# A post-norm decoder layer on one core: the first sequence's feed-forward layers issued among the second sequence's attention

## The chip, the core and the metric

One core of one Trainium2 chip runs one program. The time is that of the whole program on the device, in microseconds (us). Of the kernel before, three runs are shown: 967.42, 971.66 (the median) and 973.08.

## What is computed

Two sequences of 1024 tokens with 256 features go through one decoder layer, all in float32:

```python
x = _layernorm(x + _L0_attn_ref(x, w_qkv, w_proj))            # 16 heads of 16, rope, causal
x = _layernorm(x + _L0_xattn_ref(x, ctx, ctx, mask, ...))     # 77 context positions, 16 heads
x = _layernorm(x + _L0_ffn_ref(x, ...))
# feed-forward, D_IN = 256, D_HID = 1024
h = silu(tlin(x, w1_w, w1_s)) * tlin(x, w2_w, w2_s)
h = gelu(tlin(h, h1_w, h1_s))
h = gelu(tlin(h, h2_w, h2_s))
return tlin(h, w3_w, w3_s)
```

Here tlin(x, w, s) is x @ w.T times a scale for each output, and the weights w are small whole numbers, which need few bits of the mantissa.

## The kernel before, in words

A loop of two passes (line 338) runs one sequence each; at its end stand a barrier of all engines and a clearing of the semaphores. All weights of feed-forward, 22 pieces of 4 KB a partition, lie in SBUF in `ffn_w`. One region of SBUF, the arena, is used over and over: the tiles of attention, later those of feed-forward.

A pass has four stages, and on every engine its instructions stand in one fixed order, written out by hand as numbered steps. What joins the engines is semaphores.

- **Projections.** PE makes q and k of eight token tiles (L456) and v (L463), DVE turns q and k by rope (L980 to L982), POOL adds (L1265), ACT evicts v (L849).
- **Self-attention.** Steps -20 to 57. For each pair of heads DVE and POOL split q and k in a high and a low part (L1012, L1271), PE transposes them (`turn`, L507), ACT evicts (L843). PE makes 24 blocks of scores (`max_unit`, L521) only for the maximum of each row; DVE reduces them (L1028 whole blocks, L1030 those on the diagonal). The maxima go by PE (L528), ACT and four small DMAs (L425) into extra rows of q. Then steps 0 to 47 take one block of 128 keys for four heads each: four scores (L550) into four banks, the exponential on ACT (L878), the causal cut on POOL (L1280), the values on PE (L567). The maxima of a later pair of heads are made beside the steps of an earlier one, up to step 32. From step 42 on the output projection, norm and the next queries are made tile by tile (L591, L598, L605, L615, L1085, L1099). In the first pass DVE also looks whether a weight needs more bits than a single pass of float32r holds (L1074, 22 pieces).
- **Cross-attention.** Steps -9 to 12, in the same manner with 77 keys (L638, L655, L1124, L676, L908, L1141 and L1318 for the mask, L688, L696), then the second norm, whose result DVE and ACT split into `x_hi` and `x_lo` (L894, L1147).
- **Feed-forward** (`ffn`, L715). Two chunks of 512 tokens. Each activation is split in a high part (DVE, L1164) and a low part (POOL, L1326), and every product is made with both. Groups: w1 and w2 for eight tiles of outputs (L733), h1 and h2 with sixteen matmuls a group (L749), w3 for four token tiles (L761). Silu and Gelu are ACT's (L954, L964), the gate's product DVE's (L1224). Six banks go round. The first chunk's w1 and w2 groups run beside the last four tiles of the norm of cross-attention (L737).

PE's order in one step of self-attention is this (from line 784):

```python
for j in range(4):
    if 0 <= s < LAST:
        score(s, j)
    for unit in units[j:j + 1]:
        max_unit(*unit)
    ...                       # turn, rows, y_turn
norm_products(0, s, ("yt", "proj"))
if 0 <= s - 1 < LAST:
    values(s - 1)
norm_products(0, s, ("xt", "q"))
```

Of the kernel before, what the change touches and what calls it, by code (L numbers as in the profile page):

```python
# [20 lines left out]
F32 = mybir.dt.float32  # L22
# [79 lines left out]
SHARED = 6  # L102
# [11 lines left out]

# [28 lines left out]
def norm_bank(k, what, t):  # L144

    if k == 0:
        if t < NT // 2:
            return {"yt": 0, "proj": 1, "xt": 0, "q": 1}[what]
        return {"yt": 0, "proj": 2, "xt": 4, "q": 6}[what] + t % 2  # L150
    return {"yt": 0, "proj": 1, "xt": 0}[what] + (6 if t >= NT // 2 else 0)
# [9 lines left out]
def bank_before(k, what, t):  # L161

    uses = [u for s in range(norm_step(NT - 1) + 5) for u in norm_stages(k, s)]
    uses = [u for u in uses[:uses.index((what, t))] if norm_bank(k, *u) == norm_bank(k, what, t)]
    return uses[-1] if uses else None

def decoder_layer(nc, a):
    with ExitStack() as ctx:
# [10 lines left out]
        bias_k = sb("bias_k", [P, D], F32)  # L180
        bias_v = sb("bias_v", [P, D], F32)
# [3 lines left out]
        cos_t = sb("cos_t", [P, NT, DH], F32)  # L185
        sin_t = sb("sin_t", [P, NT, DH], F32)
# [9 lines left out]
        tok = sb("tok", [P, NT, D], F32)  # L196
        low_bits = sb("low_bits", [P, PW], U32)
# [6 lines left out]
        stats = sb("stats", [P, 2, 6], F32)  # L204
        mean_var = sb("mean_var", [P, 2, 2], F32)
        var_eps = sb("var_eps", [P, 2, 1], F32)
        rstd = sb("rstd", [P, 2, 1], F32)

        arena = (nc.sbuf_base + 31) // 32 * 32  # L210

        def at(name, shape, dt, offset):
            return nc.alloc_sbuf_tensor_at(name, shape, dt, offset=arena + offset)
# [4 lines left out]
        v_sb = at("v_sb", [P, NT, VROW], F32, O_V)  # L218
        qk_tok = at("qk_tok", [P, 2, NP, NT, 2 * DH], F32, O_QK)
        x_tok = at("x_tok", [P, NT, D], F32, O_T + 3 * 8192)  # L220
        stage = [at(f"stage_{n}", [P, NT * 2, 4, DH], F32R, O_STAGE + 4096 * i)
                 for i, n in enumerate("qk")]
        turned = [[at(f"{n}_t{b}", [P, T], F32R, O_T + 8192 * b + 4096 * i) for i, n in enumerate("qk")]
                  for b in range(QKBUF)]
        x_t = at("x_t", [P, KD, T], F32, O_T + 8192 * (QKBUF - 1))
        prob = [at(f"prob{i}", [P, CHUNK], F32, O_P + 2048 * i) for i in range(8)]
        y_sb = at("y_sb", [P, CHUNK], F32, O_Y)
        rope_a = [at(f"rope_a{i}", [P, CHUNK], F32, O_P + 2048 * i) for i in range(2)]
        rope_b = [at(f"rope_b{i}", [P, CHUNK], F32, O_P + 4096 + 2048 * i) for i in range(2)]
        w_kv = at("w_kv", [P, 2, KD, D], F32, O_P + 8192)  # L230
        ctx_t = at("ctx_t", [P, KD, CTX], F32, O_P + 12288)
        kx_tok = at("kx_tok", [P, NP, 2, DH], F32, O_P + 13312)
        y_t = [at(f"y_t{i}", [P, KD, P], F32, O_T + 4 * 8192 + 1024 * i) for i in range(2)]
        x1_t = [at(f"x1_t{i}", [P, KD, P], F32, O_T + 4 * 8192 + 2048 + 1024 * i) for i in range(2)]
        resid = [at(f"resid{i}", [P, D], F32, O_T + 4 * 8192 + 4096 + 1024 * i) for i in range(2)]
# [102 lines left out]
        with nc.Fori(0, BATCH) as b:  # L338
            with nc.Block() as block:
                build_sequence(nc, block, b, shared, S)  # L340
# [1034 lines left out]
```

## Time and profile before

| | |
|---|---|
| three runs, us | 967.42, 971.66, 973.08 |
| the profiled execution, us | 979.19 |
| its span, first to last instruction, us | 977.8 |
| mean granted clock of TensorE | 0.895 |
| busy share PE, DVE, ACT, POOL | 90%, 55%, 37%, 37% |
| DMA | 34.61 MB, 35 GB/s on average |

The profile is one execution. A busy share counts the time from an instruction's start to its modelled end, so that a string of short matmuls with waits of 0.1 us between them looks busy throughout. PEld is the loading of weights into the array, which runs beside the matmuls. PEclk is the share of full clock that TensorE was granted: 1.00 is 2.4 GHz, 0.50 is 1.2 GHz, and a figure between is a mean over a stretch. The page gives it in 40 slices:

```
PE   5879999888889999999968789999998889999997
PEclk9965999769986999999979668997999699999999
```

### The profile page before, as it was taken

To read this page: it belongs to the slowest core of one execution; us is meant where nothing else is said; L and a number is where in the kernel's file an instruction comes from. 1 tells how busy PE (TensorE), PEld (TensorE's weight loads), DVE (VectorE), ACT (ScalarE), POOL (GpSimd) and SP (SyncE) were. 2 spreads that over 40 slices of the span, in tenths; PEclk is the share of its full clock that TensorE was granted. 3 is DMA by queue.
4 is the path that set the end of the run, shared out by engine and by line. 5 is a ranking of instruction groups with operands and counts; after the bars stand their busy time and mean duration, and the time that the engine had idled before them with its cause. 6 is when DMAs were issued, how large, how long until landed. Compare 5 with 4: busy or idle time off the path is not lost. (4 is left out here: it accounts for less than half of the span.)

```text
span 977.8 us, 13145 instructions
## 1 busy us (share of the span) xinstructions
PE 882.5 (90%) x4466; PEld 563.2 (58%) x4466; DVE 538.2 (55%) x1404; ACT 364.8 (37%) x770; POOL 363.0 (37%) x576
## 2 busy tenths in 40 slices
PE   5879999888889999999968789999998889999997
PEld 2545444334644788888745444543357257888886
DVE  3596788767676711441145967886167774116113
ACT  0314666454354421231103236665734443113110
POOL 4312224345345533353333122231362645335333
PEclk9965999769986999999979668997999699999999
DMA  9909201000000000000020000010000000000000
GB/s 305 336 7 401 72 2 46 2 1 1 2 5 0 1 1 1 1 1 1 22 94 1 1 2 2 2 45 2 1 1 4 3 1 1 1 0 22 1 1 24
DMA packets 15973, 34.61 MB, mean 35 GB/s; under 512 B 3483, under 2 KB 12392, under 8 KB 15720
## 3 DMA queue, kind: packets, MB, share of 16 engines
q1 hardware_dynamic: 15896, 33.63, 9.9%
q8 instruction: 42, 0.69, 0.3%
q14 instruction: 35, 0.29, 0.1%
HBM read 31.00 MB, written 13.63 MB: 46 GB/s over the span
## 5 line engine op out<-in xcount | busy, mean ns | idle before, releaser
L749 PE MATMUL bank<-hid_lo,ffn_w 128*128 128x512 f32 x512 | 202.2, 395 | 0.0
L878 ACT ACTIVATE prob<-bank 128x512 f32<-128x512 f32 (+3 forms) x384 | 164.2, 496 | 101.6 <-PE bank L550 100.9
L749 PE MATMUL bank<-hid_hi,ffn_w 128*128 128x512 f32 x512 | 201.6, 394 | 0.0
L1326 POOL TENSOR_TENSOR hid_lo<-act_raw,hid_hi 128x512 fp32r<-128x512 f32 x96 | 123.9, 1290 | 182.4 <-DVE hid_hi L1164 182.4
L1164 DVE CAST hid_hi<-act_raw 128x512 fp32r<-128x512 f32 x96 | 41.7, 435 | 212.4 <-ACT act_raw L964 211.3
L521 PE MATMUL bank<-k_t,q_t 64*128 64x512 f32 (+3 forms) x384 | 145.0, 496 | 13.0 <-DVE max_raw L1030 8.5
L1280 POOL TENSOR_SCALAR_AFFINE_SELECT prob<-prob 128x128 f32<-128x128 f32 x256 | 84.0, 344 | 180.5 <-ACT prob L878 177.9
L1030 DVE CUSTOM_DVE_ANT_0 bank<-bank,causal_bf 128x128 f32<-128x128 f32 (+3 forms) x256 | 122.3, 512 | 28.9 <-PE bank L521 26.8
L550 PE MATMUL bank<-q_t,k_t 64*128 64x512 f32 (+3 forms) x384 | 123.8, 438 | 0.9 <-issue 0.5
L964 ACT ACTIVATE act_raw<-bank,scales 128x512 f32<-128x512 f32 x64 | 44.2, 690 | 193.1 <-PE bank L749 193.1
L550 PEld LDWEIGHTS bank<-q_t,k_t 64*128 64x128 f32 x384 | 63.3, 211 | 82.5 <-ACT prob L878 47.5
L749 PEld LDWEIGHTS bank<-hid_lo,ffn_w 128*128 128x128 f32 x512 | 95.9, 187 | 23.9
L749 PEld LDWEIGHTS bank<-hid_hi,ffn_w 128*128 128x128 f32 x512 | 95.9, 187 | 23.3
L567 PE MATMUL bank<-prob,v_sb 128*32 128x512 f32 (+3 forms) x768 | 94.3, 567 | 8.6 <-POOL prob L1280 8.3
L1028 DVE TENSOR_REDUCE max_raw<-bank 128x1 f32<-128x512 f32 x128 | 82.4, 685 | 33.6 <-PE bank L521 33.6
L521 PEld LDWEIGHTS bank<-k_t,q_t 64*128 64x128 f32 x384 | 68.3, 222 | 52.0 <-DVE max_raw L1030 27.1
L456 PE MATMUL bank<-w_qkv,x_t 128*128 128x512 f32 x64 | 35.3, 698 | 22.0 <-issue 9.7
L733 PE MATMUL bank<-x_hi,ffn_w 128*128 128x512 f32 x128 | 51.3, 400 | 2.6 <-DVE x_lo L1147 2.6
L1318 POOL TENSOR_TENSOR prob<-prob,xmask_t 77x512 f32<-77x512 f32 x32 | 39.1, 1240 | 35.4 <-ACT prob L908 35.4
L733 PE MATMUL bank<-x_lo,ffn_w 128*128 128x512 f32 x128 | 50.6, 395 | 0.0
L908 ACT ACTIVATE prob<-bank 77x512 f32<-77x512 f32 x64 | 32.7, 591 | 25.9 <-PE bank L676 25.8
L1287 POOL TENSOR_SCALAR var_eps<-mean_var 128x1 f32<-128x1 f32 x48 | 15.1, 315 | 73.2 <-DVE mean_var L1080 73.1
(127 smaller groups left out, 1234.5 us busy)
## 6 DMA issues: line engine op xcount, KB each, us to landing
ffn_w<-scratch_h SPq DMA_DIRECT2D x2, 4096.0 KB, 23.2
ffn_w<-scratch_w SPq DMA_DIRECT2D x3, 1024.0 KB, 7.0
x_t<-in_x_t SPq DMA_DIRECT2D x2, 1024.0 KB, 5.2
x_tok<-in_x SPq DMA_DIRECT2D x2, 1024.0 KB, 5.5
out<-tok SPq DMA_DIRECT2D x16, 128.0 KB, 1.8
q_t<-max_rows SPq DMA_DIRECT2D x64, 4.0 KB
qx_t<-max_rows SPq DMA_DIRECT2D x64, 4.0 KB
w_qkv<-in_w_qkv SPq DMA_DIRECT2D x1, 768.0 KB, 6.9
```

What stands on the lines that cost most here:

```text
L521: mm(out[:, 0:k1 - k0], qkt(p, 0)[r, P * qt:P * (qt + 1)], qkt(p, 1)[r, k0:k1], start=True, stop=True).then_inc(S["max_mm"], 1)
L550: mm(S_BANK[j][:, 0:CHUNK - q0], qkt(p, 1)[r, P * kb:P * (kb + 1)], qkt(p, 0)[r, CHUNK * c + q0:CHUNK * (c + 1)], start=True, stop=True).t ...
L567: m = mm(Y_BANK[32 * j:32 * (j + 1), q0:CHUNK], v_window(v_sb[:, kb], 4 * g + j), prob[4 * (s % 2) + j][:, 0:CHUNK - q0], start=kb == 0, s ...
L733: o = mm(out[:], w_view(i, dt)[:, k, P * m:P * (m + 1)], view(x_hl[part][:, k, tokens]), start=k + part == 0, stop=(k, part) == (KD - 1, 1))
L749: o = mm(out[:], w_view(2 + layer, dt)[:, k, P * m:P * (m + 1)], view(src[part][:, k]), start=k + part == 0, stop=(k, part) == (KH - 1, 1))
L878: act.activation(prob[4 * (s % 2) + j][:, 0:n], S_BANK[j][:, 0:n], ACT.Exp, scale=SCALE).then_inc(S["exp_done"], 1)
L964: act.activation(act_raw[r % 3][:], bank[n % FFN_BANKS][:], ACT.Gelu, scale=scales[:, 2 + layer, m:m + 1]).then_inc(S["ffn_act"], 1)
L1028: dve.tensor_reduce(dst, unit_bank(n)[:], AXX, ALU.max).then_inc(S["max_red"], 1)
L1030: dve.tensor_tensor_reduce(out=unit_bank(n)[:, 0:left], in0=unit_bank(n)[:, 0:left], in1=L["causal_bf"][:, CHUNK - left:CHUNK], scale=1.0, ...
L1164: dve.tensor_copy(dst, act_raw[r % 3][:]).then_inc(S["act_hi"], 1)
L1280: pool.affine_select(out=pr, in_=pr, compare_op=ALU.is_ge, fill=0.0, base=0, pattern=[[1, P]], channel_multiplier=-1).then_inc(S["select_d ...
L1326: pt(dst[1][:, r % 8], act_raw[n % 3][:], dst[0][:, r % 8].bitcast(F32), ALU.subtract).then_inc(S["act_lo"], 1)
```

## The change

The loop over the sequences is gone. Each sequence has an arena and a token tile of its own, and semaphores count on through both. The first sequence goes through projections, self-attention and cross-attention as before, but for two things: its weights are looked at in the second arena, from a DRAM copy (21 pieces in three DMAs, the last one by itself), and all engines wait for the last low part of x (`first_sequence_done`). Then comes a list of slots: the steps of the second sequence, 13 of projection, 78 of self-attention, 22 of cross-attention, and 4 more. In each, PE issues some of the first sequence's feed-forward matmuls. After the slots comes the second sequence's feed-forward as before, with Silu, six banks, and all weights in SBUF (`home`, reloaded in four portions as the first arena falls free).

```python
SLOTS = [("Q", t) for t in range(NT + V_LAG)] + [("S", s) for s in range(FIRST_STEP, S_END)] + \
        [("X", s) for s in range(-XSTAGE, FFN_STEP)] + [("E", i) for i in range(4)]
# chunk, layers, first slot, last slot, slot of a burst of Gelus, first slot of the splits
PLAN = [
    (0, ("w1", "w2"), ("Q", 2), ("Q", 12), None, None),
    (0, ("h1",), ("S", -18), ("S", -5), None, ("S", -4)),
    (0, ("h2",), ("S", 0), ("S", 27), ("S", 29), ("S", 29)),
    (0, ("w3",), ("S", 33), ("S", 37), None, None),
    (1, ("w1", "w2"), ("S", 38), ("S", 47), None, None),
    (1, ("h1",), ("S", 49), ("X", -7), None, ("X", -6)),
    (1, ("h2",), ("X", -2), ("X", 7), ("X", 8), ("X", 9)),
    (1, ("w3",), ("E", 0), ("E", 3), None, None),
]
```

The matmuls of a line are spread evenly over its slots. In a slot of self-attention their place is between the scores and the values:

```diff
-            norm_products(0, s, ("yt", "proj"))
+            f_products(slot, exact)
+            norm_products(q, 0, s, ("yt", "proj"))
             if 0 <= s - 1 < LAST:
-                values(s - 1)
+                values(q, s - 1)
```

In a slot of projection they stand between `project_qk` and `project_v`, in one of cross-attention between `x_rows` and `x_values`. They have two banks, 4 and 5:

```diff
+A_BANKS = (0, 1)
+S_BANKS = ((2, 3, 4, 5), (2, 3, 2, 3))
+Y_BANK, R_BANK = 6, 7
+QK_BANKS = (2, 3)
+V_BANKS = ((4, 5), (6, 7))
+SHARED = (6, 4)
+F_BANKS = (4, 5)
```

So the four scores of a step of the second sequence share two banks, and the maximum products of its first two pairs have four banks instead of six. The wait ahead of a score:

```diff
-            if s:
-                pe.wait_ge(S["exp_done"], 4 * (s - 1) + j + 1)
+            if S_BANKS[q][j] in S_BANKS[q][:j]:
+                wait(pe, q, name, 4 * s + j - 1)
+            elif s:
+                wait(pe, q, name, 4 * (s - 1) + max(i for i in range(4) if S_BANKS[q][i] == S_BANKS[q][j]) + 1)
```

The other engines' share, ahead of their work of the slot. The gate is made with tanh, as silu(a) = a/2 (1 + tanh(a/2)), in two products on DVE; in the h2 groups, which lie among exponentials, ACT copies and does the Gelus later in one burst:

```diff
+                if layer == "w1":
+                    act.activation(raw[m][:], out[:], ACT.Tanh, scale=half_scale[:, 0, m:m + 1]).then_inc(S["f_evac"], 1)
+                elif (c, layer) in IN_BURST:
+                    act.activation(raw[m][:], out[:], ACT.Copy).then_inc(S["f_evac"], 1)
+                else:
+                    act.activation(raw[m][:], out[:], ACT.Gelu, scale=scales[:, 1 + LAYER_NUMBER[layer], m:m + 1]).then_inc(S["f_evac"], 1)
+            for c, layer in F_BURST[slot]:
+                for m in range(KH):
+                    act.wait_ge(S["f_evac"], 24 * c + 8 * LAYER_NUMBER[layer] + m + 1)
+                    act.activation(raw[m][:], raw[m][:], ACT.Gelu, scale=scales[:, 1 + LAYER_NUMBER[layer], m:m + 1]).then_inc(S["f_gelu"], 1)
...
+                if layer == "w1":
+                    dve.scalar_tensor_tensor(out=raw[m][:], in0=raw[m][:], scalar=1.0, in1=out[:],
+                                             op0=ALU.add, op1=ALU.mult).then_inc(S["f_gate1"], 1)
+                if layer == "w2":
+                    dve.scalar_tensor_tensor(out=raw[m][:], in0=out[:], scalar=half_scale[:, 1, m:m + 1], in1=raw[m][:],
+                                             op0=ALU.mult, op1=ALU.mult).then_inc(S["f_gate2"], 1)
+                if layer == "w3":
+                    out_stats(0, 4 * c + m, out[:, 0:D])
```

DVE makes the high parts (`f_split`), POOL the low ones; both output norms have semaphores and small tiles of their own. The weights come in 44 tiles of 512 KB through a ring of six, each loaded once the group that used its place is done:

```diff
+        def fill_ring(r):
+            if r >= RING:
+                sp.wait_ge(S["f_mm"], RING_LAST[r - RING] + 1)
+            sp.dma_start(ring[r % RING][:], a["scratch"][r % PIECES]).then_inc(ring_in[r % RING], 16)
```

The branch on the weights' bits (`exact`) is taken once, ahead of the slots, instead of ahead of each feed-forward stage.

## Rows read from the trace of the kernel before

**Rows 1.** The page: busy time of each engine over the span of 977.8 us.

```profile
PE 882.5 (90%) x4466; PEld 563.2 (58%) x4466; DVE 538.2 (55%) x1404; ACT 364.8 (37%) x770; POOL 363.0 (37%) x576
```

**Rows 2.** Windows: from:to length, PE PEld DVE ACT POOL busy, PEclk, DMA share, GB/s.

```profile
324.10:494.60 170.50, 168.12 (x786) 137.26 (x786) 49.31 (x111) 39.33 (x57) 68.81 (x66) 1.00 0.03 11
350.00:375.00 25.00, 25.00 (x109) 20.04 (x108) 2.99 (x7) 4.83 (x7) 8.99 (x7) 1.00 0.00 0
504.30:533.20 28.90, 26.35 (x80) 14.71 (x80) 14.20 (x33) 5.82 (x13) 13.20 (x12) 0.90 0.01 1
533.20:570.60 37.40, 29.00 (x114) 16.88 (x115) 32.09 (x110) 7.63 (x15) 4.50 (x6) 0.69 0.01 1
570.60:595.40 24.80, 24.01 (x107) 12.34 (x111) 16.25 (x52) 13.71 (x30) 6.18 (x18) 0.57 0.01 2
595.40:667.10 71.70, 68.55 (x457) 33.33 (x449) 59.92 (x183) 47.54 (x114) 22.83 (x70) 1.00 0.05 17
667.10:682.70 15.60, 15.07 (x65) 6.13 (x65) 9.57 (x27) 7.43 (x15) 1.18 (x4) 0.67 0.00 0
682.70:717.00 34.30, 32.89 (x217) 14.22 (x213) 8.42 (x25) 24.12 (x63) 15.77 (x51) 0.95 0.01 2
717.00:735.20 18.20, 15.02 (x89) 10.47 (x87) 11.83 (x30) 4.63 (x14) 8.48 (x18) 1.00 0.00 1
735.20:756.00 20.80, 18.61 (x147) 16.68 (x148) 16.04 (x41) 10.51 (x22) 5.13 (x7) 1.00 0.02 5
756.00:786.50 30.50, 26.98 (x119) 9.36 (x123) 21.08 (x38) 15.83 (x33) 17.13 (x14) 0.61 0.01 3
786.50:801.90 15.40, 12.08 (x73) 7.61 (x65) 13.10 (x37) 5.83 (x14) 7.32 (x14) 1.00 0.01 2
```

**Rows 3.** Timeline: start, length, work, [idle before]; PE's first work in sequence 2.

```profile
504.35 2.05 PE L456 MATMUL bank<-w_qkv,x_t 128*128 128x512 f32 x2 [9.74 <-issue]
```

**Rows 4.** Timeline of DVE: low parts of the first and fourth token tile.

```profile
318.42 0.42 DVE L1147 TENSOR_TENSOR x_lo<-bank,x_hi 128x256 fp32r<-128x256 f32 x1
...
323.56 0.42 DVE L1147 TENSOR_TENSOR x_lo<-bank,x_hi 128x256 fp32r<-128x256 f32 x1
```

**Rows 5.** Timeline: most of one step of self-attention at full clock.

```profile
613.95 0.49 PE L550 MATMUL bank<-q_t,k_t 64*128 64x512 f32 x1
...
614.51 1.29 DVE L1028 TENSOR_REDUCE max_raw<-bank 128x1 f32<-128x512 f32 x2 [0.67 <-PE bank L521]
614.54 1.09 ACT L878 ACTIVATE prob<-bank 128x512 f32<-128x512 f32 x2 [0.60 <-PE bank L550]
...
614.61 0.66 PE L507 MATMUL bank<-ident,stage_q 128*128 128x128 f32 x4
...
615.20 0.50 PE L550 MATMUL bank<-q_t,k_t 64*128 64x512 f32 x1
...
615.86 0.18 PEld L521 LDWEIGHTS bank<-k_t,q_t 64*128 64x128 f32 x1 [0.30 <-DVE max_raw L1028]
...
616.17 0.43 PE L567 MATMUL bank<-prob,v_sb 128*32 128x128 f32 x8
```

**Rows 6.** Groups by form (busy us, mean ns, idle before): feed-forward's side work.

```profile
L1326 POOL TENSOR_TENSOR hid_lo<-act_raw,hid_hi 128x512 fp32r<-128x512 f32 x96 | 123.9, 1290 | 182.4 <-DVE hid_hi L1164 182.4
...
L964 ACT ACTIVATE act_raw<-bank,scales 128x512 f32<-128x512 f32 x64 | 44.2, 690 | 193.1 <-PE bank L749 193.1
...
L1164 DVE CAST hid_hi<-act_raw 128x512 fp32r<-128x512 f32 x96 | 41.7, 435 | 212.4 <-ACT act_raw L964 211.3
...
L1224 DVE SCALAR_TENSOR_TENSOR act_raw<-bank,scales,silu_sb 128x512 f32<-128x512 f32 x32 | 24.0, 750 | 17.1 <-PE bank L733 11.8 <-ACT silu_sb L954 5.0
...
L964 ACT ACT_TABLE_LOAD x4 | 5.1, 1283 | 0.1
```

**Rows 7.** The page's DMA issues: KB each, us to landing.

```profile
ffn_w<-scratch_h SPq DMA_DIRECT2D x2, 4096.0 KB, 23.2
```

**Rows 8.** Line L1141: durations in ns, min/median/max.

```profile
L1141 DVE TENSOR_TENSOR prob<-prob,xmask_t x32: 677/684/1640, 281.7 to 787.0; 77x512 f32<-77x512 f32 x32
```

More of the change, by code:

```diff
@@ L217, in decoder_layer @@
         O_Y = O_P + 16384
[L218 to L232, printed above, removed]
@@ L338, in decoder_layer @@
[L338 to L345 removed]
+        S = {n: sem(n) for n in PER}
+        for n in """check_op flag_mm flag_set f_mm f_evac f_gelu f_gate1 f_gate2 f_hi f_lo
+                 ffn_mm ffn_act ffn_gate act_hi act_lo""".split():
+            S[n] = sem(n)
@@ L475, in turn_ctx @@
             if j == 0:
-                pe.wait_ge(S["ctx_stage"], 3)
-            for q in range(4):
-                m = pe.transpose(bank[j][:, P * q:P * q + CTX], ctx_pair(4 * j + q), ident[0:CTX, 0:CTX])
+                wait(pe, q, "ctx_stage", 3)
+            for i in range(4):
+                p = 4 * j + i
+                pair = stage[q][1][0:CTX, 2 * p:2 * p + 2].rearrange("p h a e -> p (h a e)").bitcast(F32)
+                m = pe.transpose(bank[j][:, P * i:P * i + CTX], pair, ident[0:CTX, 0:CTX])
@@ new lines, in _ @@
+        pe.wait_ge(set_pool, 10)
+        pe.wait_ge(set_dve, 3)
+        wait(pe, 0, "x_t_in", 16)
+        pe.wait_ge(L["w_qkv_in"], 16)
+        for t in range(NT + V_LAG):
+            projections(0, t)
+        pe.wait_ge(w_in, 16 * 7)
+        for s in range(FIRST_STEP, S_END):
+            attention(0, s)
+        pe.wait_ge(S["check_op"], PIECES + 3)
+        wait(pe, 0, "q_add", NT)
+        mm(S_BANK[0][3][0:1, 0:1], low_max[:], L["ones"][:], start=True, stop=True).then_inc(S["flag_mm"], 1)
@@ L830, in _ @@
+        for s in range(-XSTAGE, XNORM + NT + 4):
+            if s == -XMAX:
+                pe.wait_ge(S["flag_set"], 1)
+            cross_attention(0, s)
+        first_sequence_done(pe)
+        wait(pe, 1, "x_t_in", 16)
         with pe.register("low_bits_any") as found:
@@ new lines, in _ @@
+        last = L["causal_bf"][:, CHUNK - P:CHUNK]
+        pool.affine_select(out=last, in_=last, compare_op=ALU.is_ge, fill=NEG, base=0,
+                           pattern=[[-1, P]], channel_multiplier=1).then_inc(set_pool, 1)
+        fill(0)
+        pool.memset(low_bits[:], 0).then_inc(S["check_op"], 1)
+        for t in range(NT):
+            projections(0, t)
+        pool.wait_ge(w_in, 16 * 7)
+        for s in range(FIRST_STEP, S_END):
+            attention(0, s)
+        pool.wait_ge(S["check_op"], PIECES + 3)
@@ L1321, in _ @@
+        fill(1)
+        for s in range(-XSTAGE, XNORM + NT + 4):
+            cross_attention(0, s)
+        first_sequence_done(pool)
+        for k in range(END_SLOT):
+            f_work(k)
+            stage_name, s = SLOTS[k] if k < len(SLOTS) else ("E", 0)
+            if stage_name == "Q":
+                projections(1, s)
+            if stage_name == "S":
+                attention(1, s)
+            if stage_name == "X":
+                cross_attention(1, s)
         for c in range(NC):
```

1424 lines of the change are left out of this document (847 added, 577 removed).

## The prediction, on record before the changed kernel was timed

> **What bounds it now.** The busy shares come first: PE stands at 90%, no other engine over 55% [rows 1]. That figure is a mean over two different programs, so the windows by stage come next [rows 2]. The reader should see two kinds of window. In feed-forward (324.1 to 494.6, and again at the end) PE streams without gaps: 109 matmuls in 25.00 us, 0.229 us each, at clock 1.00, with DVE, ACT and POOL at 29, 23 and 40%. In the attention of the second sequence, 504.3 to 801.9 or 297.6 us, PE is called busy too, but at clocks of 0.57 to 0.69 in four windows, and with waits between short matmuls. The timeline of one step shows these [rows 5]: two scores, maximum products and transposes up to 615.20, then the other two scores, a wait of 0.30 for DVE's reduction at 615.86, the values at 616.17, and the next step at 616.5. So the question is whether those waits lie where the change puts its matmuls.
>
> **What is removed.** The first sequence's own feed-forward stage, and the gap behind it. PE's next work after it starts at 504.35, after 9.74 us idle (stores, barrier, clearing) [rows 3]. From 324.1 to 504.3 that is 180.2 us.
>
> **What is added ahead of the overlap.** All engines wait for the last low part of x before the second sequence starts. Before, tiles 4 to 7 of the norm ran beside feed-forward. Alone they go at the pace of tiles 0 to 3: 318.42 to 323.56 is three intervals, 1.71 us each [rows 4]; four more cost 6.9 us. Flag and branch 1.5 us (an estimate; before's own branch lay in the same place). Together 8.4 us. The memsets, loads and check pieces of sequence 1 are the same in number and lie beside PE work; cover gone, the POOL memsets would cost 2 to 3 us.
>
> **What is moved.** Per sequence PE issues 640 matmuls of 512 columns and 128 of 256: 640 x 0.229 + 128 x 0.115 = 161.3 us. The plan spreads them over 13 slots of projection, 78 of self-attention, 22 of cross-attention and 4 more. PE takes them in program order, at one place of a slot, after the scores and before the values. A wait is filled only if it lies at that place. In the step of [rows 5] it does not: the maximum products wait for the two A banks, which DVE frees at 0.65 us each, and that loop runs before the moved matmuls. So I take them as nearly additive there. By stage, before to after:
> - Projections, 28.9 to 42: 64 matmuls are 14.7; about 3 of slack are filled (clock 0.90), and some 1.5 lost because each bank of the two is freed by a tanh (0.69, as the evictions of L964) and then a DVE product (0.75) [rows 6].
> - Steps -20 to -1, 37.4 to 54.5: DVE sets the pace (32.1 of 37.4 us) [rows 2], PE has real slack. 128 matmuls are 29.3; fourteen slots of 2.1 plus about 1.0 of their own are 43, the other six 11.5. This is the one stage where some 12 us are hidden.
> - Steps 0 to 29, 24.8 + 71.7 to 25 + 94: 128 matmuls, 29.3. The first six steps ran at clock 0.57 and took 24.8; at 1.00 they take about 19, like the 24 of the next window (3.0 each), and the added matmuls keep the clock up.
> - The burst and steps 30 to 32, 15.6 to 18.5: 4 come back from the clock (0.67); at step 29 eight Gelus (0.69 from PSUM, I take 0.6 from SBUF) and two table loads of 1.28 [rows 6] stand on ACT ahead of the slot's exponentials and turn evictions, 7.4 us, about 6 or 7 of them seen by PE, whose third score and values queue behind.
> - Steps 33 to 47, 34.3 to 61: 22.0 us of matmuls, 4.5 for the score banks (the third score waits for this step's first exponential; where no transposes stand between, 0.3 a step), 5 for the tanh chain at 0.5 a slot, less 4.5 of slack.
> - Steps 48 to 57, 18.2 to 37: 96 matmuls are 22.0; the norm chain's waits (4) are covered, 1 is lost at the first h1 group.
> - Cross-attention to step -1, 20.8 to 30.5: 32 + 26 matmuls, 13.2, less 4.
> - Steps 0 to 7, 30.5 to 48.5: 12.8 matmuls a slot are 2.9 us; the two pairs of scores now share two banks, so each slot has a round trip of 0.59 + 0.60 + half of 1.09 ahead of them [rows 5]; the clock (0.61) comes back. With 1.4 of values and turns that is 6.1 us a slot.
> - Steps 8 to 12, 15.4 to 25.5: the second burst, 7.4, and two splits of 1.29 a slot on POOL ahead of the norm's own.
> - The last w3 products, 64 x 0.115 and a wait for their splits: 9.
> - The second feed-forward stage, +1.5: the first banks wait for the output norm of sequence 1.
>
> The stages grow by 13, 17, 22.5, 3, 27, 19, 9.5, 18, 10, 9 and 1.5: 149.5 us. So 161.3 us of matmuls and some 40 of new waits cost 149.5; the rest is filled slack and clock.
>
> **Side work.** DVE gets 32 products of 0.75 (two for each pair now), 48 casts of 0.435 and 8 output norms of about 1.9 (an estimate, five operations of 0.2 to 0.45 by the nearest cast), 60 us [rows 6]; it was busy 202.5 us of the 297.6 (the ten windows) and comes to 262 of some 445, 59%. They stand ahead of the slot's reductions, which PE's next maximum products await; steps -20 to -1 apart, there is room. POOL gets 48 splits of 1.29, 62 us beside the 102 it has there; they stand ahead of the select that the values await, but mostly in slots without one. I take 0 beyond the terms above.
>
> **The sum.** 977.8 - 180.2 + 8.4 + 149.5 = 955.5 us of span, 956.9 with the 1.4 us that the profiled run has around its span. That run was 979.2, the median of the runs 971.7, 7.5 lower; so 949.4, I say 950. A change of 0.5% (4.9 us) is about what can be told from none.
>
> **Unknown costs.** Weight tiles: 512 KB each; 4 MB landed in 23.2 us, so 2.9 us a tile [rows 7], against 16 x 0.229 = 3.7 us of use when dense, with six tiles ahead. I take 0; if each of 42 came 1 us late it would be 42, but six in advance exclude most of that: 0 to 10. DMA issues on SP (44 ring, 22 home) lie ahead of the moves of maxima there; each such move is needed three steps later, so 0 to 5. Tanh: no run shows whether it costs a table load. I take 0; the other end is two loads of 1.28 for each of 8 products in steps 38 to 47, 20 us. 
> DVE and POOL side by side: the 32 mask products of L1141 took 0.684 in the median but 1.640 at the longest, beside POOL's [rows 8]. If each of the 48 moved splits met a DVE operation and cost it 0.96, that were 46 us on DVE, mostly off the path except in the steps before 0; I take 0, the end is 15.
> The Trainium skill (SBUF — State Buffer, Who interferes with whom) states that a POOL instruction and a DVE one with two SBUF inputs or in a two-port mode exclude each other for a whole instruction. This speaks against the change; the longest of [rows 8] agrees, the median doesn't, and by the rule the time would lie between this sum and rival D.
>
> **Rivals.**
> A, dense packing (chance 0.15): PE fills nearly every wait, and its streaming is the bound. For it: in the attention windows DVE is at 25 to 86% and ACT at 70% or less [rows 2]. Against it: the place of the matmuls in the slot. It would take 45 us off the sum: 905.
> B, beside in name only (0.12): nothing is hidden; 161.3 + 8.4 + 1.5 against 180.2 is -9, and with the bursts' 13 of waits not made up by clock +4. In the runs' terms 963 to 976, say 969. For it: PE 90% busy.
> C, slower (0.20): the score banks. With four banks the scores of a step run ahead of the exponentials; with two, ACT and PE hand over in turn: 0.59 from score to exponential and 0.60 of exponential, twice a step. If each of the 48 steps costs 0.75 us more than taken, with the F evictions of ACT ahead of its exponentials, that is +36: 986. It decides from 0.56 us a step. For it: in steps 33 to 47 ACT is busy 24.1 of 34.3 us, the highest share. Against: turns and maximum products lie between the scores in 33 of 48 steps.
> D, the shared port of DVE and POOL (0.03): 46 us on DVE, seen by PE for 30: 980.
>
> **Chances.** My forecast has 0.50, with a range of its own of 925 to 972. Faster by over 0.5% (below 966.8): 0.46 of it, A, and part of B: 0.65. Within: the rest of mine and most of B, 0.12. Slower (above 976.5): C and D, 0.23. The range: down to A's 905 less its lower half, so 910; up to C's middle with the ends of tanh and tiles, 990.
>
> **What would show it.** Right: the second sequence's first projection at about 332; its attention, projections to last w3 product, some 445 us long; steps 6 to 28 at 4.1 us on average instead of 3.0; clock 1.00 nearly throughout; two stretches of about 6 us without PE work where ACT shows table loads; steps -20 to -1 at 50 to 58 us; the last stage again 170 to 172 us. Wrong toward A: steps of 3.4 us, the stretch under 400. Wrong toward C: PE idle before the third and fourth score over 0.5 us a step beside transposes. Wrong altogether: PE waiting on ring tiles, table loads by the dozen, or a late start of sequence 2.

## Result, and the profile after

The changed kernel takes 997.29 us (median of 4 runs, 994.44 to 1000.71) beside 972.31 us (967.42 to 973.08) for the kernel before on the same chip: ratio 1.027, 95% interval 1.022 to 1.032, 2.7% slower. The forecast was 950, faster. The profiled execution spans 992.7 us (before: 977.8). One profile used below, that of the run with four shares, is of a slow execution (1119.6 us, granted clock 0.870; the other three of that kernel took 1076.9 to 1080.5 at 0.897 to 0.903), so its pattern is read and not its lengths.

The page of the changed kernel: busy time by engine, and the first DMA issues (KB each, us to landing).

```profile
PE 869.8 (88%) x4466; PEld 553.7 (56%) x4466; DVE 559.3 (56%) x1422; ACT 376.6 (38%) x788; POOL 363.5 (37%) x575
...
ring_s<-scratch SPq DMA_DIRECT2D x44, 512.0 KB, 3.3
home_s<-scratch SPq DMA_DIRECT2D x22, 512.0 KB, 6.1
```

The shares of [rows 1] have hardly moved, though some 161 us of dense TensorE work now lie inside another stage. That is the first sign: had the work filled waits, PE's share would have risen.

The windows of the second sequence in the changed kernel, columns as in [rows 2]; the cuts are projections, steps -20 to -1, 0 to 5, 6 to 28, 29 to 32, 33 to 46, 47 to 57, cross-attention to step -1, 0 to 6, 7 to the last w3 product, last feed-forward.

```profile
328.00:381.10 53.10, 41.93 (x144) 26.34 (x144) 30.99 (x57) 9.48 (x20) 20.48 (x16) 0.92 0.18 60
381.10:443.50 62.40, 55.24 (x242) 37.56 (x243) 38.49 (x118) 14.60 (x24) 14.39 (x14) 0.88 0.21 68
443.50:470.50 27.00, 26.33 (x139) 14.36 (x138) 16.25 (x52) 14.93 (x32) 6.97 (x19) 0.89 0.06 21
470.50:566.60 96.10, 93.11 (x548) 48.94 (x544) 58.64 (x180) 50.76 (x118) 23.16 (x70) 1.00 0.15 47
566.60:589.10 22.50, 13.58 (x72) 5.35 (x68) 14.99 (x39) 16.60 (x27) 11.00 (x11) 0.77 0.04 17
589.10:656.60 67.50, 58.50 (x337) 33.82 (x333) 26.36 (x63) 30.73 (x70) 26.75 (x66) 1.00 0.15 48
656.60:699.50 42.90, 40.71 (x202) 32.30 (x202) 14.44 (x35) 10.28 (x22) 11.47 (x21) 1.00 0.39 135
699.50:735.60 36.10, 30.44 (x195) 26.77 (x193) 22.42 (x50) 13.54 (x26) 16.10 (x15) 0.95 0.11 32
735.60:782.90 47.30, 41.76 (x204) 24.00 (x203) 16.53 (x33) 18.49 (x35) 16.46 (x14) 1.00 0.14 46
782.90:819.30 36.40, 26.21 (x154) 19.40 (x154) 24.82 (x62) 14.47 (x27) 20.57 (x27) 0.95 0.29 107
819.30:987.30 168.00, 164.50 (x788) 137.72 (x786) 52.25 (x119) 38.88 (x56) 70.68 (x70) 1.00 0.11 41
```

The stretch from the first projection to the last w3 product is 491.3 us, forecast 445 [before, without the moved work: 297.6]. The clock came back for the greater part: 1.00 in five windows, 0.88 to 0.95 in five, 0.77 in that of the burst, where [rows 2] has 0.57 to 0.69 in four. Steps 6 to 28 take 4.2 us each, as foretold (4.1). By stage the 46 us too many are 11 in the projections, 8 before step 0, 8 in steps 0 to 32, 12 in steps 33 to 57, 6 in cross-attention before its step 0. From there to the last w3 product it is 83.7 us, forecast 83.

One step of self-attention in the changed kernel, timeline of PE (start, length, work, idle before):

```profile
470.56 0.50 PE L684 MATMUL bank<-q_t_s,k_t_s 64*128 64x512 f32 x1
470.56 0.73 PE L649 MATMUL bank<-k_t_s,q_t_s 64*128 64x512 f32 x2
...
471.23 0.66 PE L635 MATMUL bank<-ident,stage_q_s 128*128 128x128 f32 x4
...
472.29 0.49 PE L684 MATMUL bank<-q_t_s,k_t_s 64*128 64x512 f32 x1
472.47 0.38 PE L649 MATMUL bank<-k_t_s,q_t_s 64*128 64x256 f32 x1
472.79 0.50 PE L880 MATMUL bank<-hid_f_hi_s,ring_s 128*128 128x512 f32 x1
473.12 0.39 PE L880 MATMUL bank<-hid_f_lo_s,ring_s 128*128 128x512 f32 x1
```

The moved products (L880) come after all scores (L684) and maximum products (L649). A score and the maximum product beside it, on the other 64 rows, start at the same time (470.56): this becomes important below.

The burst of step 29, timeline of ACT, DVE, POOL and PE:

```profile
566.95 1.28 ACT L1152 ACT_TABLE_LOAD   x1
...
568.25 5.01 ACT L1152 ACTIVATE raw_s<-raw_s,scales 128x512 f32<-128x512 f32 x8
...
569.51 1.27 POOL L1660 TENSOR_TENSOR hid_f_lo_s<-raw_s,hid_f_hi_s 128x512 fp32r<-128x512 f32 x1 [6.56 <-DVE hid_f_hi_s L1471]
569.61 1.45 DVE L1471 CAST hid_f_hi_s<-raw_s 128x512 fp32r<-128x512 f32 x1 [0.18 <-ACT raw_s L1152]
...
573.27 1.28 ACT L1103 ACT_TABLE_LOAD   x1
574.57 1.09 ACT L1103 ACTIVATE prob_s<-bank 128x512 f32<-128x512 f32 x2
575.22 0.79 PE L684 MATMUL bank<-q_t_s,k_t_s 64*128 64x512 f32 x1 [7.38 <-ACT prob_s L1103]
```

ACT is held for 7.6 us (forecast 7.4), and PE waits 7.38 us ahead of the third score (forecast 6 or 7).

A step without transposes between the scores (steps 33 to 46):

```profile
606.00 0.87 ACT L1103 ACTIVATE prob_s<-bank 128x384 f32<-128x384 f32 x2 [1.92 <-PE bank L684]
...
606.54 0.82 PE L684 MATMUL bank<-q_t_s,k_t_s 64*128 64x384 f32 x2 [0.64 <-ACT prob_s L1103]
```

The third score waits for the first exponential of its own step, since it shares that score's bank.

### The profile page after: what moved, and what is told of

It reads as the page before. It is cut to its first block, busy times and chain, and to the rows that moved or that the text cites. A ratio compares the mean times of both kernels' runs of the same rounds, so it can differ in the third digit from the quotient of the medians.

```text
span 992.7 us, 13083 instructions
## 1 busy us (share of the span) xinstructions
PE 869.8 (88%) x4466; PEld 553.7 (56%) x4466; DVE 559.3 (56%) x1422; ACT 376.6 (38%) x788; POOL 363.5 (37%) x575
## 4 chain that ended last, share of the span: by engine, by line
PE 73%; DVE 12%; POOL 5%; ACT 5%; issue 3%; DMA 1%; SPq 0%; POOLq 0%; DVEq 0%; ACTq 0%
PE bank L880 13%; PE bank L946 11%; PE bank L684 8%; PE bank L701 7%; PE bank L649 5%; PE bank L635 3%; PE bank L584 3%; PE bank L867 3%; DVE bank L1300 3%; PE bank L928 2%; PE bank L823 2%; DVE max_raw L1298 2%; PE bank L811 2%; ACT prob_s L1103 2%; PE bank L734 1%
## 5 line engine op out<-in xcount | busy, mean ns | idle before, releaser
L1103 ACT ACTIVATE prob_s<-bank 128x512 f32<-128x512 f32 (+3 forms) x384 | 166.4, 494 | 131.3 <-PE bank L684 129.0
L1633 POOL TENSOR_SCALAR_AFFINE_SELECT prob_s<-prob_s 128x128 f32<-128x128 f32 x256 | 83.9, 343 | 178.4 <-ACT prob_s L1103 175.9
L649 PE MATMUL bank<-k_t_s,q_t_s 64*128 64x512 f32 (+3 forms) x384 | 135.6, 461 | 14.4 <-DVE max_raw L1300 11.3
L684 PE MATMUL bank<-q_t_s,k_t_s 64*128 64x512 f32 (+3 forms) x384 | 127.7, 431 | 21.5 <-ACT prob_s L1103 21.0
L684 PEld LDWEIGHTS bank<-q_t_s,k_t_s 64*128 64x128 f32 x384 | 61.5, 200 | 108.5 <-ACT prob_s L1103 64.4
L880 PE MATMUL bank<-hid_f_hi_s,ring_s 128*128 128x512 f32 x256 | 105.7, 413 | 0.5 <-DVE qk_tok_s L1372 0.5
L880 PE MATMUL bank<-hid_f_lo_s,ring_s 128*128 128x512 f32 x256 | 104.2, 407 | 0.0
L946 PE MATMUL bank<-hid_hi_s,home_s 128*128 128x512 f32 x256 | 99.7, 390 | 0.0
L946 PE MATMUL bank<-hid_lo_s,home_s 128*128 128x512 f32 x256 | 99.7, 390 | 0.0
L701 PE MATMUL bank<-prob_s,v_sb_s 128*32 128x512 f32 (+3 forms) x768 | 88.4, 534 | 8.0 <-POOL prob_s L1633 7.1
L1660 POOL TENSOR_TENSOR hid_f_lo_s<-raw_s,hid_f_hi_s 128x512 fp32r<-128x512 f32 x48 | 63.2, 1328 | 73.7 <-DVE hid_f_hi_s L1471 73.6
L649 PEld LDWEIGHTS bank<-k_t_s,q_t_s 64*128 64x128 f32 x384 | 62.2, 204 | 47.5 <-DVE max_raw L1300 23.0
L880 PEld LDWEIGHTS bank<-hid_f_hi_s,ring_s 128*128 128x128 f32 x256 | 49.0, 191 | 14.2 <-issue 3.9
L880 PEld LDWEIGHTS bank<-hid_f_lo_s,ring_s 128*128 128x128 f32 x256 | 48.8, 191 | 11.5 <-issue 2.3
```

Of the source, the lines that this page charges most:

```text
L649: mm(out[:, 0:k1 - k0], qkt(q, p, 0)[r, P * qt:P * (qt + 1)], qkt(q, p, 1)[r, k0:k1], start=True, stop=True).then_inc(S["max_mm"], 1)
L684: mm(S_BANK[q][j][:, 0:CHUNK - q0], qkt(q, p, 1)[r, P * kb:P * (kb + 1)], qkt(q, p, 0)[r, CHUNK * c + q0:CHUNK * (c + 1)], start=True, sto ...
L701: m = mm(Y[32 * j:32 * (j + 1), q0:CHUNK], v_window(v_sb[q][:, kb], 4 * g + j), prob[q][4 * (s % 2) + j][:, 0:CHUNK - q0], start=kb == 0, ...
L880: o = mm(out[:], view(tile_h(tile[:], k), True), view(hid_f[part][:, k]), start=i == 0, stop=i == last)
L946: o = mm(out[:], weight(tile_h(home[PIECE_H[layer] + m][:], k)), view(src[part][:, k]), start=k + part == 0, stop=(k, part) == (KH - 1, 1))
L1103: act.activation(prob[q][4 * (s % 2) + j][:, 0:n], S_BANK[q][j][:, 0:n], ACT.Exp, scale=SCALE).then_inc(S["exp_done"], 1)
```

## Experiments

Two terms of the sum could be wrong, and one assumption: the price of two score banks in place of four; the price of ACT's, DVE's and POOL's side work; and that products at one place of a slot fill nothing. The first three runs build the kernel up part by part; each of them was timed once.

**Two banks, no moved work.** The second sequence keeps the changed kernel's banks, its partner's feed-forward is gone.

```
+F_MM, F_BURST, F_SPLIT, F_AFTER, F_FINISH = ([[] for _ in range(END_SLOT)] for _ in range(5))
```

> The feed-forward layers of the first sequence are left out on every engine (its output is its x before them); the second sequence keeps its two shared score banks and four banks for the maxima, and all weight tiles are loaded at once. Theory 1 (two score banks make the third score wait for an exponential of the same step, also without any side work): the 468 us of the second sequence in the kernel before come back as 493 to 498, so with a start at 328 the run takes 821 to 832. Rival (the banks cost nothing by themselves, the new waits come from the side work of ACT and DVE): 798 to 804.

Measured: 824.9 us, as theory 1 has it.

**Four banks, no moved work.**

```
-S_BANKS = ((2, 3, 4, 5), (2, 3, 2, 3)); SHARED = (6, 4)
+S_BANKS = ((2, 3, 4, 5), (2, 3, 4, 5)); SHARED = (6, 6)
```

> The same, the feed-forward layers of the first sequence left out, with the four score banks and six banks for maxima of the kernel before. Both theories: 328 + 468 + what lies after, 798 to 804, with the stages of the second sequence as long as in the kernel before within 2 us. The difference to the run with two banks is the whole price of the banks: 25 to 30 us by theory 1, under 4 by its rival.

Measured: 791.3 us, 7 below the lower end (steps 0 to 32 came out 6 us and the last stage 4 us shorter than before), and 33.6 below the run with two banks, somewhat over the 25 to 30. Windows of both: steps 0 to 28 and 33 to 40 with two banks,

```profile
395.80:488.00 92.20, 87.43 (x555) 42.84 (x555) 74.00 (x232) 60.43 (x141) 28.82 (x88) 0.94 0.05 13
502.20:527.10 24.90, 20.68 (x106) 8.22 (x102) 1.81 (x6) 12.34 (x33) 7.96 (x28) 0.64 0.01 2
```

and with four:

```profile
392.70:484.30 91.60, 87.80 (x556) 43.59 (x556) 74.20 (x232) 59.79 (x141) 28.85 (x88) 0.94 0.05 14
498.40:512.50 14.10, 12.75 (x105) 5.26 (x101) 1.83 (x6) 9.91 (x31) 7.77 (x28) 1.00 0.01 3
```

Steps 0 to 28 pay 0.6 us in all, steps 33 to 40 10.8, 1.35 a step (some of it the clock, 0.64). Where maximum products and transposes stand between the second score and the third, they cover the exponential; where nothing does, the hand-over is bare.

**Products alone.** PE issues all moved products, ACT, DVE and POOL do nothing for them.

> The feed-forward products of the first sequence run on TensorE in their slots, with the streamed weight tiles, but ACT, DVE and POOL do nothing for them (no tanh, gates, Gelu, splits or norms; the products of the hidden layers read a copy of x; the output of that sequence is its x before the layers). Theory 3 (products at one place of a slot fill no wait; 157 us of them at full clock, less some 22 us that the higher clock gives back): 135 us above the run with two banks and no feed-forward layers, 956 to 967, so that side work is worth 30 to 40 us of the 997. Rival (the products would fill the waits if it were not for the side chains): 915 to 935, side chains 60 to 80 us. A third reading, side work free: 985 or more.

Measured: 952.4 us. Products cost 127.6 us over the run with two banks. That is 3.6 under theory 3's lower end, and far from both rivals; side work is the other 44.9 of the 997.3, more than its 30 to 40. By span the ledger closes: 977.8 before, -188.3 without the moved work (789.5), +33.6 for banks, +127.5 for products, +42.1 for side work, 992.7.

By stage, lengths from the traces (us, cut at the stage's first product):

| stage | 4 banks | 2 banks | + products | + side work | halves (below) |
|---|---|---|---|---|---|
| projections | 28.7 | 28.7 | 41.4 | 53.1 | 53.3 |
| -20 to -1 | 37.4 | 40.7 | 56.3 | 62.4 | 62.5 |
| 0 to 28 | 91.6 | 92.2 | 123.6 | 123.1 | 111.1 |
| 29 to 32 | 14.1 | 14.1 | 15.6 | 22.5 | 24.2 |
| 33 to 46 | 32.6 | 52.1 | 66.9 | 67.5 | 60.1 |
| 47 to 57 | 18.6 | 19.4 | 41.5 | 43.0 | 43.0 |
| cross -9 to -1 | 21.9 | 20.8 | 28.8 | 36.1 | 35.4 |
| cross 0 to 6 | 29.0 | 36.8 | 50.4 | 47.3 | 40.0 |
| cross 7 to last w3 | 16.9 | 19.6 | 25.9 | 36.4 | 35.0 |

Steps 0 to 28 grow by 31.4 us for 128 products of 0.229, 29.3 us, though DVE is busy only 61% and ACT 53% of the changed kernel's window there: wholly additive.

**Four shares a slot.** If PE's order alone is at fault, deal the products out.

```
                 if 0 <= s < LAST:
                     score(q, s, j)
+                f_products(slot, exact, j, 4)
                 for unit in units[j:j + 1]:
                     max_unit(q, *unit)
...
-            f_products(slot, exact)
```

> The changed kernel, with the products of a slot dealt out in four shares, one behind each score (behind each maximum unit or cross-attention score) and not all at one place. Theories 1 and 3 (the waits for shared banks, some 30 us, and part of those for maxima stand idle only because TensorE's order puts nothing there): 20 to 35 us less, 962 to 977. Rival (the bound lies in ACT's and DVE's chains, so order on TensorE matters little): 990 to 1000. Against: products ahead of a score could make ACT wait for scores, then over 1000.

Measured: 1080.5 us, ratio 1.110 (1.105 to 1.115), 83 us worse than what it was to mend. Timeline of PE in one step:

```profile
512.61 0.79 PE L684 MATMUL bank<-q_t_s,k_t_s 64*128 64x512 f32 x1
513.33 0.80 PE L881 MATMUL bank<-hid_f_hi_s,ring_s 128*128 128x512 f32 x1
514.05 0.79 PE L649 MATMUL bank<-k_t_s,q_t_s 64*128 64x512 f32 x1
514.65 0.63 PE L684 MATMUL bank<-q_t_s,k_t_s 64*128 64x512 f32 x1
515.20 0.79 PE L881 MATMUL bank<-hid_f_lo_s,ring_s 128*128 128x512 f32 x1
```

Score and maximum product no longer start together, and before and behind the first moved product stand 0.72 us from start to start, in a stretch at the lower of the clock's two levels, 1.2 GHz. At 2.4 GHz, start to start at the median: 0.230 us between two moved products, 0.42 from a 64-row product to a moved one, 0.33 back, and 0.004 between a score and its partner where the step doesn't part them (the run with halves, below). So a product of 128 rows between two of 64 breaks their running side by side and pays for two changes of shape. The Trainium skill (TensorEngine Tiling (Array Packing), Tiling Modes, Key Properties) says that changing the tiling mode drains the engine, and that different tiles run in parallel; these rows agree with both. How much of the 83 us is the parting itself, and how much the lower clock that came with it, the runs do not tell apart.

**Two shares.** So the second share has to stand where the shape changes anyway: behind the transposes, ahead of the third score.

```
             for j in range(4):
+                if two and j == 2:
+                    f_products(slot, exact, 0, 2)
...
-            f_products(slot, exact)
+            f_products(slot, exact, int(two), 1 + two)
```

> The changed kernel, but half of a slot's products stand ahead of the third score (no pair of scores or maximum units is parted), the other half at the old place, in every step that has scores. The run with four shares took 1080, and its timeline shows why: a 64-row product and its partner on the other 64 rows start together (0.004 us apart at the median), and a 128-row product between them parts the pair and costs 0.09 to 0.2 us at each side. Theory (the wait ahead of the third score is real idle time, and products there fill it if they part no pair): steps 33 to 46 of the second sequence from 67.5 to 53 to 58 us, X0 to 6 from 47.3 to 40 to 43, steps 0 to 28 from 123.1 to 127 to 132, because there is no such wait and each new place costs two changes of shape; in all 980 to 990. Rival (exponentials then come later and the next step waits instead): 33 to 46 still 65 or more, in all 997 to 1010.

Measured: 967.1 us, ratio 0.990 (0.987 to 0.994): 30 us less than the changed kernel, and faster than the kernel before. More than expected, but not where expected: cross 0 to 6 fell to 40.0 as foreseen, steps 33 to 46 only to 60.1 (53 to 58 expected), and steps 0 to 28 fell by 12.0 where I had them grow. Its timeline:

```profile
492.56 1.29 DVE L1305 TENSOR_REDUCE max_raw<-bank 128x1 f32<-128x512 f32 x2 [1.33 <-PE bank L649]
...
492.65 0.66 PE L635 MATMUL bank<-ident,stage_q_s 128*128 128x128 f32 x4
493.06 0.47 PE L882 MATMUL bank<-hid_f_lo_s,ring_s 128*128 128x512 f32 x1
493.38 0.39 PE L882 MATMUL bank<-hid_f_hi_s,ring_s 128*128 128x512 f32 x1
...
493.69 0.49 PE L684 MATMUL bank<-q_t_s,k_t_s 64*128 64x512 f32 x1
493.70 0.38 PE L649 MATMUL bank<-k_t_s,q_t_s 64*128 64x256 f32 x1
```

Two products run while DVE reduces the first two maxima (to 493.85); the third maximum product then has its bank almost at once and starts beside its score. The wait I had put "before the moved matmuls" is met by moving them there.

**Spare banks.** Scores three and four take the maximum products' banks in steps 33 to 40 and cross 1 to 5 of the changed kernel.

```
+        spare = 1 <= s <= XNORM - 1 if cross else 33 <= s <= 40
+        return (2, 3, 0, 1)[j] if q and spare else S_BANKS[q][j]
```

> The changed kernel, but the third and fourth score go to the two banks of the maximum units in the steps in which these have nothing to do (33 to 40 of self-attention, 1 to 5 of cross-attention). From the two runs without side work, two banks cost 10.7 us in steps 33 to 40 and 7.8 us in X0 to 6: theory 1 gives steps 33 to 40 from 32.9 to 21 to 24 us and X0 to 6 from 47.3 to 40 to 43, in all 978 to 985. Rival (with products in the step anyway, the wait only moves to the values): under 5 us in all, 992 to 998.

Measured: 980.1 us, ratio 1.005 (1.002 to 1.008). Steps 33 to 40 from 32.9 to 24.7 (24 at most expected), cross 0 to 6 from 47.3 to 40.1: theory 1. The bank waits stay real with products in the step.

**Burst without Gelu.**

> The changed kernel, but the two bursts of eight Gelu are copies, so that ACT loads no tables for them (the Gelu of the second hidden layer of the first sequence is left out). Theory (the burst's 6.9 us in steps 29 to 32 come mainly from ACT being held: 2 loads of 1.28 us and 8 passes of about 0.6 us): 1.5 to 3 us less in steps 29 to 32 (22.5 to 19.5 to 21), as much around X8, in all 991 to 994. Rival (the eight splits on DVE and POOL behind it set the time): no change in steps 29 to 32, 995 to 999.

Measured: 989.4 us (one run), 1.6 under the theory's range. Steps 29 to 32 from 22.5 to 18.9, cross 7 on from 36.4 to 34.9: the loads and the longer passes are 3.6 of the 6.9 us that the first burst costs over products alone; the rest was not taken apart.

**Other slots.**

> The same products in other slots: both hidden layers of the first half of the tokens before step 0, its last layer and the gated and first hidden layer of the second half in steps 4 to 31, none in steps 33 to 47 and X0 to 8, where the scores have four banks again; one burst, in step 48, where no exponential is due. By the runs so far: 29.5 us of the 33.6 for the banks come back, one burst of some 7 us is gone and the other costs less, the products cost what they cost anywhere (0.245 us each): 955 to 965, some 1% faster than the kernel before. Rival (side work bound: 18 products a slot before step 0 with eight Gelu and splits delay the maxima): 970 to 985.

Measured: 987.7 us, ratio 1.014 (1.010 to 1.018), above even the rival's 985. Steps 33 to 46 fell to 34.1 as expected, but steps -20 to -1 grew to 96.1 for twice the products, and 0 to 28 to 150.2: some 45 us of products there, with their side work, cost 58 us over the run without any. What is moved out of a bank wait loses the cover that the wait gave it: in steps 33 to 46, 21.0 us of products (58 x 0.229 + 64 x 0.12) had cost 14.8. And what is moved into a stage whose slack is used up finds none: before step 0 the first 128 products had cost 15.6 us, and 6.1 for their side work; the second 128 cost 33.7 with theirs. How much of that is side work was not taken apart.

**Three edits together.**

Halves also in the steps before 0, the spare banks, and a shorter stretch for the gated layer:

```
-    (0, ("w1", "w2"), ("Q", 2), ("Q", 12), None, None),
+    (0, ("w1", "w2"), ("Q", 5), ("Q", 12), None, None),
```

> Three edits on the changed kernel together: half of a slot's products ahead of the third score or maximum unit, now in the steps before 0 too; the third and fourth score in the banks of the maximum units where these have nothing to do; and the gated layer of the first half of the tokens in Q5 to Q12 and not Q2 to Q12, since in Q0 to Q7 DVE has the rotation as well. From the run with halves (967): 4 to 7 us less by the second edit (steps 33 to 40 from 27.9 to 23 to 25, X0 to 6 from 40.0 to 37 to 39), 4 to 7 less in steps -20 to -1 (62.5 to 56 to 58), 5 to 8 less in Q (53.3 to 45 to 48): 947 to 956, 2% faster than the kernel before. Rival (the gains overlap, Q is bound by the chain from TensorE over ACT and DVE and back): 960 to 967.

Measured: 979.2 us, ratio 1.008 (1.005 to 1.011), worse than halves alone. Projections 63.4 and not 46; steps -20 to -1 64.5; the spare banks gave 0.8 us in steps 33 to 40 and nothing in cross 0 to 6, where halves had already taken 5.0 and 7.3. All three expectations missed.

**Four shares between the pairs.**

> The run with halves (967), but in steps up to 32 the products of a step stand in four shares, ahead of the second, third and fourth score and at the old place, so that a score and the maximum unit behind it stay neighbours. In the run with four shares of 1080 us each share stood between the two, and steps 0 to 28 took 226.7 us (halves: 111.1). Theory (it was the parted pairs): steps 0 to 28 take 110 to 122 us, the clock stays up, in all 966 to 978. Rival (every change between 64-row and 128-row products costs so much, however placed): steps 0 to 28 take 160 us or more, in all over 1010.

Measured: 987.2 us (one run), nearer to the theory, 9 above its range. By the runs' times, 93 of the 113 us between halves and four shares are gone with the pairs kept whole (the four shares also parted products before step 0 and in cross-attention, so not all of the 93 belong to these steps). But steps 0 to 28 take 136.1 us, 25 more than with halves: 0.43 us for each of the two further places in 29 steps.

**All in the middle.**

> As the combination of three edits, but all products of a slot with scores or maximum units stand ahead of the third score, none at the old place. If the waits in the middle of a step (maxima on DVE, shared banks) are the larger ones: 3 to 8 us less than the combination. If the wait for the exponentials ahead of the values is then open again: 3 to 10 us more. I expect the second, as the third and fourth exponential are then asked for later.

Measured: 978.8 us, ratio 1.007 (1.003 to 1.010): no difference to the combination; neither case.

**The gated layer's chain.** What did the plan with Q5 to Q12 lengthen? In the run with halves, late in the projections (timeline of ACT, DVE and PE):

```profile
365.75 0.38 ACT L1081 ACTIVATE v_sb_s<-bank 128x256 f32<-128x256 f32 x1 [3.54 <-PE bank L591]
...
366.03 0.68 ACT L1151 ACTIVATE raw_s<-bank,half_scale 128x512 f32<-128x512 f32 x1
366.75 0.69 DVE L1487 SCALAR_TENSOR_TENSOR raw_s<-raw_s,bank 128x512 f32<-128x512 f32 x1 [2.57 <-ACT raw_s L1151]
...
367.49 0.50 PE L869 MATMUL bank<-x_hi_s,ring_s 128*128 128x512 f32 x1 [1.54 <-DVE raw_s L1487]
```

The tanh of a group long finished stands behind the copy of V, and that waits for the last product of the slot. Each slot then pays the whole chain tanh, gate, next group.

```
-F_AFTER = [[n for n in range(len(GROUPS)) if F_DONE[n] == k - 1] ...
+F_AFTER = [[n for n in range(len(GROUPS)) if k == F_DONE[n] + (F_DONE[n] > LAST_Q)] ...
```

> The run with halves (967), with the spare banks, and with the chain of the gated layer taken up sooner in Q: ACT's tanh of a slot's group stands ahead of the copy of V of the same slot (and no longer behind it, which waits for the slot's last product), DVE's products behind the rotation of that slot. Theory (Q's 11.7 us over the run with products alone are this order: at 366.03 a tanh starts only behind the V copy at 365.75, and TensorE waits 1.54 us for what follows): Q from 53.3 to 43 to 47, the rest as in the run with halves less 1 for the banks, in all 956 to 961. Rival (Q is bound by DVE's work, rotation 1.5 and gates and cast 1.9 us a slot, or POOL's port): Q 50 to 53, in all 964 to 968.

Measured: 962.3 us, ratio 0.989 (0.984 to 0.995). Projections 47.4 and the total are 0.4 and 1.3 us over the theory's upper ends; the stage is clear of the rival's 50 to 53. The tanh now starts ahead of the V copy:

```profile
367.71 0.69 ACT L1161 ACTIVATE raw_s<-bank,half_scale 128x512 f32<-128x512 f32 x1
...
368.56 0.38 ACT L1091 ACTIVATE v_sb_s<-bank 128x256 f32<-128x256 f32 x1 [0.16 <-PE bank L596]
```

The runs do not tell this kernel from the one with halves (0.989 and 0.990, intervals overlapping); the stage does. The projections got 5.9 of their 11.7 us of side work back. PE's four waits for the first gate product, 5.7 us together, are down to one of 0.6. The rest is one wait at the end of the stage, the same in both kernels; in the changed kernel (timeline of ACT, DVE, POOL and PE):

```profile
375.95 0.68 ACT L1144 ACTIVATE raw_s<-bank,half_scale 128x512 f32<-128x512 f32 x1
...
378.68 1.38 POOL L1660 TENSOR_TENSOR hid_f_lo_s<-raw_s,hid_f_hi_s 128x512 fp32r<-128x512 f32 x1 [3.59 <-DVE hid_f_hi_s L1471]
378.85 1.49 DVE L1281 CAST stage_k_s<-qk_tok_s 128x512 fp32r<-128x512 f32 x1
...
381.15 1.09 PE L635 MATMUL bank<-ident,stage_q_s 128*128 128x128 f32 x4 [5.52 <-DVE stage_k_s L1286]
```

DVE makes q and k ready for the first transposes (L1281, L1286) only behind the last group's chain.

**Products alone, halves.**

> As the run with products on TensorE alone (952; no tanh, gates, Gelu, splits or norms for the first sequence's feed-forward layers, whose output is its x before them, and the hidden layers' products read a copy of x), with half of a slot's products ahead of the third score. If the gain of that order (30 us with side work) is that of TensorE's own order: 920 to 930, and the side work costs the same 40 to 45 us in either order. If it is rather that side work came at a better time: 940 to 952.

Measured: 916.8 us (one run), 35.6 less than products at one place and 3.2 below the expected range. The order's gain is TensorE's own. Side work costs 50.3 us over it (967.1), more than the 40 to 45 expected.

## Why the prediction was wrong

The span came out at 992.7 us, forecast 955.5. (The other 10 of the 47 us between 950 and 997 are no mechanism: the profiled execution before lay 7.5 above its runs' median, this one 2.9 below.) The order of the argument was right: the work stands at one place of a slot, what stands there fills few waits, and two banks and side work are paid on top. Three prices were wrong, each by some 15 us.

**Removed, added ahead: right, and somewhat better.** The second sequence starts at 328.0, forecast 332; the last stage takes 168.0, forecast 170 to 172. Without the moved work the span falls by 188.3, forecast 171.8. Some 7 of that are stages that became shorter by themselves (290.8 us, before 297.6).

**The score banks: the step that failed first.** I took "4.5 for the score banks, 0.3 a step" in steps 33 to 47 and a round trip in cross 0 to 7, 13.9: 18.4 in all. Measured are 33.6. Steps 33 to 46 alone pay 19.5 (1.4 a step), steps -20 to -1 3.3 and cross-attention from step 0 on 10.5. The mechanism was named, and rival C even placed its strongest evidence there, but priced it at 0.75 over all 48 steps. The runs say: next to nothing where transposes and maxima stand between the scores, about twice my rival's price where none do. Rival C's 986 is the nearest of the forecasts to 997, and that is partly luck: it gave the banks all of its 36 us, and they are 15 of the excess. Its sign, long waits beside transposes, did not show.

**Side work: the step that failed second.** "I take 0 beyond the terms above", and those terms (tanh, bursts, the splits at the end) come to some 27 us. It is 42: projections 11.7 (I had 1.5), steps -20 to -1 6.1 (0), the first burst 6.9 (6 to 7, right), steps 33 to 57 2.1 (6), cross -9 to -1 7.3 (0), from cross 0 on 7.4 (some 12). So it was too low in three stages and too high in two. I had costed by durations, a tanh of 0.69 and a product of 0.75, and not by where they stand in the order of ACT, DVE and POOL. In the projections that order is nearly the whole: 5.7 us of waits for the gate product, nearly gone where the tanh stands ahead of the V copy, and 5.5 ahead of the first transposes. In cross -9 to -1, PE waits three times, 5.7 us together, for the low part of the staged q, which POOL makes behind two moved splits; with products alone it does not wait for it at all (timeline of POOL and PE, changed kernel):

```profile
708.29 2.79 POOL L1660 TENSOR_TENSOR hid_f_lo_s<-raw_s,hid_f_hi_s 128x512 fp32r<-128x512 f32 x2 [3.02 <-DVE hid_f_hi_s L1471]
711.05 0.72 POOL L1686 TENSOR_TENSOR stage_q_s<-qk_tok_s,stage_q_s 128x256 fp32r<-128x256 f32 x1
711.82 1.56 PE L774 MATMUL bank<-ident,stage_q_s 128*128 128x128 f32 x8 [1.82 <-POOL stage_q_s L1686]
```

**Products: additive as said, but not as much was filled.** By the prediction's own terms the new waits come to 45.6 us (its text says some 40), so of 149.5 products were to cost 104 net, with slack and clock. They cost 127.5. Seven us of the clock and slack came back without them, so 17 were taken too low: in steps 0 to 32 I had 10 us filled or given back, and it is 3; in cross-attention from step 0 on 19, and it is 11. "This is the one stage where some 12 us are hidden": from two banks to products alone, steps -20 to -1 grew by 15.6 for 29.3, so 13.7 were. And "the maximum products wait for the two A banks, and that loop runs before the moved matmuls" is what the run with halves confirms from the other side.

**Port of DVE and POOL: small in sum, but some of it on the path.** Of 48 casts of the moved work the median is 0.422 us, seven take 0.94 to 1.45, some 4.6 us more in all. Of the 24 casts that stage the second sequence's q and k, seven take 0.67 to 1.50 where 0.42 to 0.52 is usual, some 6 us more; with products alone, where POOL makes no splits, none is longer than 0.52. Each of these fourteen starts while a POOL instruction of 1.26 to 1.44 us runs and ends 0.28 us behind its end; a cast that starts first keeps its 0.42. The Trainium skill (SBUF — State Buffer, Who interferes with whom) has the later one blocked for the whole instruction; these casts agree. Two of them, 1.48 us each (435.68, 437.08), lie in PE's longest wait within steps -20 to -1, 3.81 us, and the one at 378.85 in the wait ahead of the first transposes. No run took the port away, so its whole part in the 42 us stays open.

## What to carry to other kernels

Before work is moved beside other work on an in-order engine, name the place in the program at which each wait lies: a wait is filled by what stands directly ahead of it, and one choice of place was worth 30 us here. Fill where the shape of the products changes anyway, since a full-row product between two half-row ones costs both their parallel run and two changes. What the guest takes from the host (two PSUM banks) is priced step by step where nothing else stands between producer and consumer, by its bare round trip. And look at what each helping engine does next for the host: a moved split or gate ahead of the cast that starts the host's next stage is a wait, however idle that engine is on average.

## What the runs showed that I had not expected

- Two 64-row products on different rows start 0.004 us apart at the median in the run with halves. A 128-row product starts 0.42 us behind a 64-row one, and the next 64-row one 0.33 behind it, at 2.4 GHz; two 128-row ones follow at 0.230.
- The clock fell where pairs were parted, and not with the number of places: the granted clock of the whole run is 0.917 to 0.927 with halves, 0.897 to 0.903 in three runs with four shares inside the pairs, and 0.932 in the one with four shares between them. PE had the same products to make in each.
- After a table load the first Gelu starts 0.02 us behind its end (566.95 + 1.28 and 568.25), and the load 0.02 us behind the last exponential (564.66 + 2.27): here the switch costs ACT no more than the load.
